# Where the scans of a fused Mamba and mixture-of-experts kernel put their states: PSUM for the steps that VectorE weighs, or the SBUF ring for all

## The reference

```
def step(state, inp):
    d, b, c, u = inp                        # per time step
    dA = jnp.exp(d[..., None] * A)          # [batch, channel, state]
    state = state * dA + (d * u)[..., None] * b[:, None, :]
    y = jnp.einsum('bdn,bn->bd', state, c)
    return (state, y)
...
x = x + y_gated                             # y + D*u, times silu(z)
x = x + moe(layernorm(x)) + shared(layernorm(x))
```

## Time and profile before

| | us |
|---|---|
| median of 3 executions | 994.5 |
| profiled execution | 992.26 |
| its span, first to last instruction | 990.5 |
| VectorE busy in the span | 590.1 (60%) |
| GpSimd busy | 582.7 (59%) |
| ScalarE busy | 494.9 (50%) |
| TensorE busy (matmuls) | 840.3 (85%) |

### The profile page before, as it was taken

The page is one execution under the profiler, slowest core; times in us unless marked ns, Lnnn a source line. Parts: engine busy times, 40 slices in busy tenths (PEclk is TensorE's granted clock), DMA queues, the critical chain, the costliest instruction groups (busy, mean ns, idle before and its releaser), DMA issues.

```text
span 990.5 us, 12614 instructions
## 1 busy us (share of the span) xinstructions
PE 840.3 (85%) x4237; PEld 470.3 (47%) x4237; DVE 590.1 (60%) x846; ACT 494.9 (50%) x893; POOL 582.7 (59%) x326
## 2 busy tenths in 40 slices
PE   6456565657989989999997999999999888989984
PEld 3244454446554565557554654444444443444441
DVE  4599998989999999999996741222222111111111
ACT  4777857687688778897761332222222111222120
POOL 0299999899999999999979311222222122222211
PEclk9578776679999999999998999999999999999997
DMA  8734353255342543435575688999999999999994
GB/s 272 265 130 147 127 173 127 86 182 176 134 163 93 209 158 138 139 136 167 173 276 180 246 324 308 384 394 397 395 390 393 397 396 395 397 397 385 398 383 93
DMA packets 68410, 250.65 MB, mean 253 GB/s; under 512 B 10506, under 2 KB 13078, under 8 KB 68092
## 3 DMA queue, kind: packets, MB, share of 16 engines
q1 hardware_dynamic: 54740, 226.09, 60.0%
q0 software_dynamic: 7712, 18.88, 7.8%
q10 hardware_dynamic: 5896, 4.90, 1.5%
HBM read 230.67 MB, written 19.17 MB: 252 GB/s over the span
## 4 chain that ended last, share of the span: by engine, by line
PE 41%; DMA 17%; POOL 15%; DVE 11%; issue 8%; SPq 4%; ACT 3%; POOLq 0%; DVEq 0%; ACTq 0%
PE ps L1031 11%; POOL arena L1673 8%; PE ps L823 7%; DMA arena<-bc_rows 7%; PE ps L1055 6%; PE ps L839 6%; PE ps L828 6%; DMA arena<-in_L_ffn_w_down 5%; POOL arena L1678 5%; SPq L714 4%; DVE ps L1427 3%; DVE arena L1434 2%; DVE arena L1427 2%; DVE arena L1455 2%; DMA out_rows<-routes,idxs 1%
## 5 line engine op out<-in xcount | busy, mean ns | idle before, releaser
L1673 POOL TENSOR_TENSOR arena<-arena 128x1024 f32<-128x1024 f32 x128 | 299.6, 2363 | 56.3 <-DMA arena<-bc_rows 51.1
L823 PE MATMUL ps<-ident,arena 128*128 128x128 f32 (+2 forms) x1408 | 222.2, 311 | 77.8 <-POOL arena L1678 30.1
L823 PEld LDWEIGHTS ps<-ident,arena 128*128 128x128 f32 (+2 forms) x1408 | 190.2, 171 | 162.4 <-issue 77.7
L1235 ACT ACTIVATE ps<-arena,An 128x511 f32<-128x511 f32 x256 | 165.0, 681 | 80.3 <-DVE ps L1435 61.5
L1427 DVE TENSOR_TENSOR_SCAN ps<-ps,arena 128x1024 f32<-128x1024 f32 x74 | 168.1, 2287 | 8.9 <-POOL arena L1673 7.0
L1687 POOL DMA_INDIRECT arena<-xn_rows,idu x32 | 34.0, 1064 | 235.4 <-DVE wcol L1583 193.2
L1031 PE MATMUL ps<-arena 128*64 128x352 f32 x984 | 159.0, 461 | 7.6 <-issue 6.5
L828 PE MATMUL ps<-xnT,sw 128*128 128x512 f32 x320 | 145.2, 598 | 2.6 <-ACT arena L1196 1.6
L1678 POOL TENSOR_TENSOR arena<-arena 128x1024 f32<-128x1024 f32 x54 | 126.7, 2359 | 2.3 <-DVE arena L1427 2.3
L1427 DVE TENSOR_TENSOR_SCAN arena<-ps,arena 128x1024 f32<-128x1024 f32 x54 | 122.4, 2281 | 5.2 <-ACT ps L1235 3.7
L1590 DVE TENSOR_TENSOR arena<-arena,ps 128x352 f32<-128x352 f32 x32 | 16.7, 521 | 170.2 <-PE ps L1031 170.2
(11 more groups left out here) (167 smaller groups left out, 909.0 us busy)
## 6 DMA issues: line engine op xcount, KB each, us to landing
arena<-bc_rows SPq DMA_DIRECT2D x128, 512.0 KB, 4.6
arena<-in_L_ffn_w_down SPq DMA_DIRECT2D x59, 768.0 KB, 23.2
arena<-in_L_ffn_w_gate SPq DMA_DIRECT2D x64, 704.0 KB, 23.5
arena<-in_L_ffn_w_up SPq DMA_DIRECT2D x59, 704.0 KB, 23.4
arena<-in_x SPq DMA_DIRECT2D x4, 1024.0 KB, 7.4
xn_rows<-xn ACTq DMA_DIRECT2D x4, 1024.0 KB, 8.5
out_rows<-arena SPq DMA_DIRECT2D x4, 1024.0 KB, 5.5
extra<-in_L_ffn_w_up SPq DMA_DIRECT2D x5, 704.0 KB, 23.1
```

Of the source, the lines that this page charges most:

```text
L823: return nc.tensor.matmul(dst, src, ident[0:k, 0:k], is_transpose=True, **kw)
L1235: a = nc.scalar.activation(ps[:, 2 * (c % 2) + n, 1:L], dt[k][:, 1:L], ACT.Exp, scale=An[:, k, NB * g + n:NB * g + n + 1])
L1673: G.tensor_tensor(R[c % RING], dtu[k][:, None, :].to_broadcast([P, NB, L]), Brep[n % REPS], ALU.mult)\
```

## The change

Every scan now writes its states into the ring buffer `R` in SBUF, whoever weighs them. VectorE's weighing reads `R` and `Crep`, both in SBUF, and writes `R` in place. The decay's PSUM pair is only read by the scan, so column 0 stays 0: the memset is gone, and with it the wait of VectorE for its own weighing. ScalarE's decay waits for the scan of two steps back in all cases. The weighing signals `cs_odd` itself. The table of who weighs what, the order of all other instructions, and everything behind the first half are as they were.

```diff
                     if c >= 2:
-                        if by_vector(c - 2):
-                            act.wait_ge(s["cs_odd"], vector_weighs(c - 2))
-                        else:
-                            act.wait_ge(s["scan_done"], c - 1)
+                        act.wait_ge(s["scan_done"], c - 1)
...
                     pair = flat(ps[:, 2 * (q % 2):2 * (q % 2) + 2, :])
-                    V.tensor_tensor_scan(pair if by_vector(q) else flat(R[q % RING]), pair, flat(R[q % RING]), 0.0,
-                                         ALU.mult, ALU.add).then_inc(s["scan_done"], 1)
+                    V.tensor_tensor_scan(flat(R[q % RING]), pair, flat(R[q % RING]), 0.0, ALU.mult, ALU.add).then_inc(s["scan_done"], 1)
...
-                    h = 2 * (q % 2)
-                    link(V.tensor_tensor(R[q % RING], ps[:, h:h + 2, :], Crep[n % REPS], ALU.mult))
-                    V.memset(ps[:, h + 1, 0:1], 0.0).then_inc(s["cs_odd"], 1)
+                    V.tensor_tensor(R[q % RING], R[q % RING], Crep[n % REPS], ALU.mult).then_inc(s["cs_odd"], 1)
```

## The result

The changed kernel took 1064.47 us (median of 4 executions, 1063.24 to 1066.92) beside 995.01 us for the kernel before; the ratio is 1.0695, 95% interval 1.0655 to 1.0735. It is 69 us slower, where +83.5 (1078 us) was forecast. Timed once more against the kernel before, it gave 1.0728 [1.0682, 1.0773].

The account below looks back on a forecast made before the run. GpSimd, busy 96.1% of the scan stretch, was taken as the bound there. Terms 0 + 0 + 76 + 12 - 5 = 83 us gave 1078 us against the 994.5 us median; range 1025 to 1145 us.

Parts of the forecast that it names:

- One sign that I had named as speaking against me: Scan stretch: the prediction is wrong if VectorE, not GpSimd, is the busier engine there.
- Memset and its wait at nothing: VectorE, between weighing and next scan: removal saves 14.8 us of VectorE, about 0 on the path, as GpSimd covers it.
- ScalarE's earlier start at nothing: ScalarE's decay waits for the scan, not the weighing and memset behind it: put at 0, up to -4.7 us.
- Scan to SBUF at nothing: VectorE's 74 scans that wrote PSUM now write SBUF: 6 ns each, 0.4 us, counted as nothing.
- Price of a meeting: GpSimd's loss when its instruction meets a VectorE weighing with two SBUF inputs: 0.92 to 1.22 us, 71 times, 76 us.
- VectorE's waiting: Weighings held by GpSimd's instructions: 71 x 1.04 = 74 us on VectorE, which stays behind GpSimd at 534 us.
- Disorder: Scan stretch: late weighings delay the scans behind them in fixed order; bounds 0 and 59 us, taken as 12.
- idle time used up: Scan stretch: the later pace uses some of GpSimd's 19.8 us idle; bounds 0 and -20, taken as -5 us.
- The second half keeps its length: Behind the scan stretch: it moves as much as the last scan does, its length unchanged at about 436 us.
- no lock: Rival: weighings and GpSimd's products run side by side as before, 988 us, faster; chance 0.05.
- part payment: Rival: contention costs half of the 76 us, hidden in GpSimd's waits or finer-grained; about +35, 1030 us; chance 0.09.
- The third: Rival: GpSimd's next instruction takes memory before the waiting weighing, making VectorE the bound; +193, about 1188 us; chance 0.08.

Follow-up runs that it names:

- crossed pair: Two kernels: the changed one with VectorE's weighing reading PSUM instead of Crep, 991.32 us; the kernel before with it reading the ring buffer instead of PSUM, 1068.72 us.

## Why the prediction was right

The direction, the place and the mechanism (weighings and GpSimd's instructions hold each other) came out; the size was 14 us too large (+83.5 against +69.5). In the traces the scan stretch grew by 72.4 us where 83 was forecast; the rest of the 14 is that the two profiled executions differ by 5 us more than the medians, less 2.3 us of the second half. One sign that I had named as speaking against me came true all the same (VectorE is the busier engine, by 2 us), and that GpSimd alone sets the end is not shown.

- *Memset and its wait at nothing.* Held: 0.9981 [0.996, 1.0002] when they go without the contention, +2 us (not told from 0) when they come back with it.
- *ScalarE's earlier start at nothing.* In the end it held: the scans wait 2.0 us for it now, 4.7 before. But I had said that ScalarE's waits for VectorE would fall well below 61.5 us. They rose from 79.7 us (memset and scans) to 111.2: the memset is gone from its path, yet the scans themselves came later.
- *Scan to SBUF at nothing.* Held, 2274 ns against 2281 and 2287, and the run with one SBUF input isolates it.
- *Price of a meeting, 0.92 to 1.22 us, taken at 1.07, 71 times, 76 us.* Here is the mis-sized term: it measured 0.98 us for the clean ones and 66.4 us in all, over 66 products and 3 casts. The lower end was nearer: it was worked out from the handovers of one meeting, the upper end was simply a weighing's whole length, and I took the middle. Against the whole 1.22 us the trace shows 0.24 less: VectorE starts 0.13 ahead of GpSimd's recorded end, and GpSimd is not held to VectorE's recorded end.
- *VectorE's waiting, 74 us.* The 74 weighings took 90.1 us in all before and 181 now, so it measured 91 us. I had put a weighing at a random point of a product. In truth the two engines fall into step: a second weighing in a row is held by a product that has just got in, and 12 of the 74 start within 0.1 us of one's start. I had also taken the whole 14.8 us of the memset off VectorE's busy time, part of which was idle; in the run where ScalarE sets the zero its busy time is 7.8 us lower (467.0 against 474.8). So VectorE is busy 557.8 us (475 + 91 - 8) of 581.5 and GpSimd 555.7: I had 534 and GpSimd alone as the bound. Here the reasoning failed, though the time did not. Both engines are 96% busy now, and the page's chain leans more on VectorE (18% against 12%). How much of the 69 us came to the end by GpSimd's loss and how much by VectorE's waiting no run separates; that GpSimd's 66.4 us and the end agree so well may in part be luck.
- *Disorder +12, idle time used up -5, together +7.* GpSimd's idle time grew by 6.0. The wait of 9.18 us ahead of the 121st product stayed, at 7.80 us, so little idle time was used up; waits for scans rose from 2.3 to 10.7 us. That the two parts were right singly is not shown.
- *The second half keeps its length.* 439.0 against 436.7 us; 2.3 us off.

Of the rivals, no lock fell with the crossed pair. A part payment fell with the size (66.4 us on GpSimd, where it had 38) and, as to the finer grain, with the weighing in two pieces. The third, GpSimd passing a waiting weighing, does happen, one or two times in a run, not 71 times: in the changed kernel a weighing was issued at 237.88 and took 8.88 us, while four products ran behind one another without a gap:

```profile
236.38 9.28 POOL L1667 TENSOR_TENSOR arena<-arena 128x1024 f32<-128x1024 f32 x4
...
237.88 8.88 DVE L1429 TENSOR_TENSOR arena<-arena 128x1024 f32<-128x1024 f32 x1
```
